# Weighting an expert's output before it is scattered instead of after it is gathered

## The chip, the cores and the metric

The kernel runs on one core of one Trainium2 chip. The metric is the device time of one launch in microseconds. The engines are TensorE (PE, its weight loads PEld), VectorE (DVE), ScalarE (ACT), GpSimd (POOL) and SyncE (SP), which only issues DMAs here. Each engine works through its own list of instructions in order; between engines there are semaphores alone. POOL and SP both issue DMAs, POOL those that scatter rows by an index.

## The reference, cut to what matters

Input x is 4 x 1024 tokens of 256 features in fp32. The kernel computes x + attention(xn) * silu(moe(xn)), with xn the layer norm of x. The mixture of experts is what the change touches:

```python
probs = softmax(x @ gate_w)                      # 8 experts
gate_score, gate_idx = top_k(probs, 2)
gate_score = gate_score / sum(gate_score)
combine = einsum('tk,tke->te', gate_score, onehot) * alpha
h = gelu(einsum('th,ehi->eti', x, fc1_w) + fc1_b)
y = einsum('eti,eih->eth', h, fc2_w) + fc2_b
out = einsum('eth,te->th', y, combine)
```

So each token has two experts, and its output is the sum of their two outputs, each with one weight (score times the expert's alpha). The weight can be multiplied in anywhere after the second bias and before the sum.

## The kernel before, in words

Everything is written out by hand for each engine; no scheduler or planner changes the order. A tile is 128 tokens (rows on the partitions) of 256 features; there are 32 tiles of tokens.

**Attention**, up to about 521 us of the profiled execution, is a sequence of windows (one for four heads of one batch element), in which PE, ACT and DVE share the work. Beside it POOL routes the tokens: it puts the two weights of each token in `weight` (L830) and the two slots in `slot` (L839), and scatters each normalised token twice into `xs_dram`, grouped by expert (`scatter`, L867 to L879). A row of `xs_dram` is 257 words: word 0 is the row of `y_dram` to which the expert's output goes back, copied ahead of the features by L871, and 256 words are the features. Rows that pad an expert's last tile lead to spare rows of `y_dram`.

**The expert loop** runs over 71 tiles of 128 grouped rows (`SLOTS`). SP loads a tile (`load_tile`, L663, four buffers `x_move`). For a tile n, PE transposes it (L1672), ACT takes it to SBUF (L1000), PE makes the hidden layer (L1689), DVE adds the first bias (`h_evacuate`, L1365), ACT does the gelu (L1004), PE makes the output (L1711), DVE adds the second bias (`y_evacuate`, L1405), and POOL scatters the 128 rows into `y_dram` by their row numbers (L903). DVE copies the row numbers out of a tile's buffer (`take_row`, L1359), and only then may SP load the tile four further into that buffer (L662). The loop is skewed: in one round DVE does `take_row(n+3)`, `h_evacuate(n+2)`, `y_evacuate(n)`, and PE transposes n+3, makes the hidden layer of n+2 and the output of n. `ysb` holds eight output tiles; a ninth waits until the first is stored. POOL also multiplies the attention output by inverse sums in 24 of the 71 rounds (`normalise`, L859).

**The last stage** works on 16 pairs of token tiles. `y_dram` has a token's two expert rows side by side. When all scatters have landed, SP loads eight pairs of `ya` (L703) and issues each further load in turn with the stores of the result (L717), behind the waits for `gsum_done` and `fin_done`. For a pair m, ACT multiplies the first expert's rows by their weight into `gsum` (`scale_first`, L1031, two instructions, two pairs ahead of the silu); DVE multiplies the second by its weight and adds (`add_second`, L1420, two instructions); ACT does the silu (L1037); PE has meanwhile made the output projection of attention in one of four banks (L1732, L1737); DVE multiplies the two (`product`, L1430) and adds x (`add_input`, L1435); SP stores. DVE's order in a round is `product(m)`, `add_second(m+2)`, `add_input(m)`. PE may begin pair m once `product(m-4)` has freed its bank.

Of the kernel before, what the change touches and what calls it, by code (L numbers as in the profile page):

```python
# [11 lines left out]

P = 128
B, T, D = 4, 1024, 256
W = D + 1
H, HD = 16, 16
E = 8
KT = D // P
# [129 lines left out]
CH = 4  # L148
# [75 lines left out]
    return isinstance(q, int) and q == NQ - 1  # L224


def in_turn(ahead, what):

    for m in range(AHEAD_OF_PRODUCT):
        ahead(m)  # L230
    for m in range(NT // 2):
        what(m)
        if m + AHEAD_OF_PRODUCT < NT // 2:
            ahead(m + AHEAD_OF_PRODUCT)


def attention_moe_kernel(nc, x, wqT, wkT, wvT, woT, qb, kb, vb, ob, gate, w1, b1, w2, b2, alpha,
                         ident_f, ident_b, mask_neg, mask_negT, before, k_rows, q_rows, numbers, empty_rows, out):
    x_t = x.rearrange("b (t p) d -> p (b t) d", p=P)
# [3 lines left out]
    with ctx:  # L243
# [48 lines left out]
        weight = sb("weight", [P, NT, 2])  # L292
        slot = sb("slot", [P, NT, 2], i32)
        tile_expert = sb("tile_expert", [P, SLOTS], i32)
        y_row_of = sb("y_row_of", [P, SLOTS], i32)
        y_row = sb("y_row", [P, NT, 2], i32)
        blank = sb("blank", [P, W])
        zeros = blank[:, 1:W]
        pad_slot = sb("pad_slot", [P, E], i32)
        spare_f = sb("spare_f", [P, E, 2])  # L300
        spare = sb("spare", [P, E, 2], i32)
        ARENA = 16 * 1024 + CH
        arena = sb("arena", [P, ARENA])
        at = [0]

# [50 lines left out]
        b1_sb = cut(E * D).rearrange("p (e n) -> p e n", e=E)  # L356
        b2_sb = cut(E * D).rearrange("p (e n) -> p e n", e=E)
        at[0] = 0
        xg = [x_move[:, j, 1:W] for j in range(CH)]
        at[0] = 0  # L360
        xgT = [cut(D) for _ in range(CH)]
        w1_now = [cut(KT * D).rearrange("p (k n) -> p k n", k=KT) for _ in range(2)]
# [91 lines left out]
        xg_in = [sem(f"xg_in{n}") for n in range(CH)]  # L454
        t1_done = sem("t1_done"); xgT_out = sem("xgT_out"); l1_done = sem("l1_done"); h_out = sem("h_out")
        g_done = sem("g_done"); w1_ready = sem("w1_ready"); l2_done = sem("l2_done")
        y_out = sem("y_out"); y_stored = [sem(f"y_stored{n}") for n in range(STEP)]
        x_all_in = sem("x_all_in"); a_in = [sem(f"a_in{b}") for b in range(B)]
        ya_in = [sem(f"ya_in{n}") for n in range(DEEP_Y)]
        vb_turned = sem("vb_turned"); vb_out = sem("vb_out"); vb_done = sem("vb_done"); ob_step = sem("ob_step"); ob_split = sem("ob_split"); s_proj = sem("s_proj"); y_scaled = sem("y_scaled")  # L460
        gsum_done = sem("gsum_done"); silu_done = sem("silu_done"); sg_done = sem("sg_done")
        fin_done = sem("fin_done"); stored = sem("stored")

# [19 lines left out]
            return bass.AP(ap.tensor, ap.offset, [list(ap.ap[0]), [0, n]] + [list(x) for x in ap.ap[1:]])  # L483

        def many_zeros(n):
            return bass.AP(zeros.tensor, zeros.offset, [list(zeros.ap[0]), [0, n], [1, D]])

        best, first, second, gap, gexp, where, norm, low = col

# [230 lines left out]

        @block.gpsimd
        def _(pool):
            nc.gpsimd.memset(zeros, 0.0).then_inc(zeros_set, 1)
            for rows in (key_rows, query_rows):
                nc.gpsimd.memset(rows[:, :], 0.0).then_inc(masks_clear, 1)
            pool.wait_ge(masks_clear, 2)
# [140 lines left out]
            def scatter(q, k):  # L867
                r = q - MOVE_FROM
                first_tile, count = MOVES[r], MOVES[r + 1] - MOVES[r]
                pool.wait_ge(scattered, 16 * (2 * first_tile + k * count))  # L870
                nc.gpsimd.tensor_copy(x_move[:, 0:count, 0:1].bitcast(i32),  # L871
                                      y_row[:, first_tile:first_tile + count, k:k + 1]).then_inc(rows_ready, 1)
                pool.wait_ge(rows_ready, 2 * r + k + 2)
                for s in range(count):
                    pool.wait_ge(exp_done, NU * q + BETWEEN_BATCHES[k][s] + SCORE_BANKS + 1)
                    nc.gpsimd.indirect_dma_start(  # L876
                        out=xs_dram, in_=x_move[:, s, :], in_offset=None,
                        out_offset=bass.IndirectOffsetOnAxis(ap=slot[:, first_tile + s, k:k + 1], axis=0)
                        ).then_inc(scattered, 16)  # L879

            for q in range(MOVE_FROM, NQ - 1):
                r = q - MOVE_FROM
                if q > MOVE_FROM and q <= FIRST_TAIL:
                    scatter(q - 1, 1)
                    pool.wait_ge(scattered, 16 * 2 * MOVES[r])
                if q < FIRST_TAIL:
                    first_tile, count = MOVES[r], MOVES[r + 1] - MOVES[r]
                    pool.dma_start(x_move[:, 0:count, 1:W], xn_t[:, first_tile:first_tile + count, :]).then_inc(x_moved, 16)
                next_v(q, q % AUG)
                if PADS_FROM <= q < PADS_FROM + E:  # L890
                    clear_pads(q - PADS_FROM, q)
                if q < FIRST_TAIL:
                    pool.wait_ge(x_moved, 16 * r + 16)
                    scatter(q, 0)
# [3 lines left out]
            for n in range(SLOTS):  # L898
                if n in NORMALISE_BESIDE:
                    normalise(*NORMALISE_BESIDE[n])  # L900
                pool.wait_ge(row_taken, n + 1)
                pool.wait_ge(y_out, n + 3)
                nc.gpsimd.indirect_dma_start(  # L903
                    out=y_dram, in_=ysb[n % STEP], in_offset=None,
                    out_offset=bass.IndirectOffsetOnAxis(ap=y_row_of[:, n:n + 1], axis=0)).then_inc(y_stored[n % STEP], 16)


        @block.scalar
        def _(act):
# [112 lines left out]

            nc.scalar.activation(std[:, :], veps[:, :], ACT.Silu)

            def scale_first(m):
                j = m % DEEP
                act.wait_ge(ya_in[m % DEEP_Y], 16 * (m // DEEP_Y) + 16)
                if m >= DEEP:
                    act.wait_ge(sg_done, m - DEEP + 1)
                for i in range(2):  # L1030
                    ins = nc.scalar.activation(gsum[j][:, i * D:(i + 1) * D], ya[m % DEEP_Y][:, i, 0, :], ACT.Identity,  # L1031
                                               scale=weight[:, 2 * m + i, 0:1])
                ins.then_inc(y_scaled, 1)

            def silu(m):
                act.wait_ge(gsum_done, m + 1)
                nc.scalar.activation(gsum[m % DEEP], gsum[m % DEEP], ACT.Silu).then_inc(silu_done, 1)  # L1037

            in_turn(scale_first, silu)


        @block.vector
        def _(dve):
            dve.sem_inc(piece_used, PIECE_BANKS)
            dve.sem_inc(h_out, 2)
            dve.sem_inc(y_out, 2)

            def statistics(i, b, c):
                if i == 1:
# [306 lines left out]

            def take_row(n, j):
                dve.wait_ge(xg_in[j % CH], 16 * (n // CH) + 16)
                nc.vector.tensor_copy(y_row_of[:, bass.ds(n, 1)], x_move[:, j % CH, 0:1].bitcast(i32)).then_inc(row_taken, 1)  # L1359


            def h_evacuate(n, j):
# [31 lines left out]
            def y_evacuate(n, j):  # L1394
                if n == INVERT_BESIDE:
                    dve.wait_ge(sums_in, 32)
                    invert_sums(B - 1)
                if n == TURN_BIAS + 2:
                    dve.wait_ge(vb_turned, 1)
                    nc.vector.tensor_copy(vb_wide, bank(4)[:, 0:D]).then_inc(vb_out, 1)  # L1400
                e = dve.value_load(tile_expert[0:1, bass.ds(n, 1)], min_val=0, max_val=E - 1)
                dve.wait_ge(l2_done, n + 1)
                if n >= STEP:
                    dve.wait_ge(y_stored[j % STEP], 16 * (n // STEP))
                nc.vector.tensor_tensor(ysb[j % STEP], bank(6 + j % 2)[:, 0:D], b2_sb[:, e, :], ALU.add).then_inc(y_out, 1)  # L1405
                if n >= SPLIT_BESIDE:
                    next(splitting, None)

# [5 lines left out]

            def add_second(m):
                j = m % DEEP
                dve.wait_ge(y_scaled, m + 1)
                for i in range(2):
                    part = gsum[j][:, i * D:(i + 1) * D]
                    ins = nc.vector.scalar_tensor_tensor(part, ya[m % DEEP_Y][:, i, 1, :], weight[:, 2 * m + i, 1:2],  # L1420
                                                         part, ALU.mult, ALU.add)
                ins.then_inc(gsum_done, 1)

            def product(m):
                j = m % DEEP
# [23 lines left out]
        def _(pe):  # L1449
# [244 lines left out]
            def expert_out(n, j):  # L1694
                e = chosen[2]
                if n == 0:
                    pe.wait_ge(o_out, 2 * NQ)
                if n == TURN_BIAS:
                    for k in range(KT):
                        ins = nc.tensor.transpose(bank(4)[:, k * P:(k + 1) * P], vb_sb[:, k * P:(k + 1) * P], idf[:, :])  # L1700
                    ins.then_inc(vb_turned, 1)
                if n == TURN_BIAS + 4:
                    pe.wait_ge(vb_out, 1)
                    for k in range(KT):
                        ins = nc.tensor.matmul(bank(5)[:, 0:D], vb_wide[:, k * P:(k + 1) * P], wo_sb[:, k, :],
                                               start=(k == 0), stop=(k == KT - 1))
                    ins.then_inc(vb_done, 1)
                pe.wait_ge(g_done, n + 1)
                pe.wait_ge(y_out, n + 1)
# [15 lines left out]
            pe.wait_ge(y_out, SLOTS + 2)  # L1725
# [80 lines left out]
```

## Time and profile before

| what | us |
|---|---|
| three runs | 709.43, 714.72, 719.42 |
| median of the runs | 714.72 |
| the profiled execution | 710.94 |
| its span, first to last instruction | 709.1 |
| expert loop in it, from about | 521 |
| last expert tile's bias add on DVE | 664.1 |
| first pair of the last stage reaches ACT | 672.7 |

The profiled execution's own time is 1.84 us longer than its span. Times in the views are microseconds from the start of the span. An engine's "idle before" is how long it stood still ahead of an instruction, with what ended the wait. Durations of successive DVE instructions overlap a little, since one starts while the other drains; so the cost of one in a full queue is the distance from its start to the next start.

### The profile page before, as it was taken

Reading aid. Unit: us, or ns where it says so; the run is one execution under the profiler, and the core shown is the slowest. Engines: PE = TensorE matmul, PEld = TensorE weight load, DVE = VectorE, ACT = ScalarE, POOL = GpSimd, SP = SyncE. Lnnn points to the kernel's source line nnn. Section 1 sums busy time; section 2 is a strip of 40 time slices with the busy share of each in tenths; the row PEclk is TensorE's granted clock in tenths of the full one; section 3 lists DMA queues with packets and bytes.
Section 4 is the critical chain, followed back from the end, with each engine's and each line's share of the span. In section 5 each row is a group of like instructions: output and inputs, shape, how many; then the busy total and the mean of one; then the engine's idle time right before and its main releaser. Section 6 shows DMA issues by size and latency. Waiting matters only on the chain.

```text
span 709.1 us, 17536 instructions
## 1 busy us (share of the span) xinstructions
PE 681.8 (96%) x6039; PEld 461.3 (65%) x6042; DVE 536.7 (76%) x1146; ACT 484.6 (68%) x994; POOL 236.1 (33%) x336
## 2 busy tenths in 40 slices
PE   6998999999999999999999999999999999999885
PEld 3885676455555556555555655554479899999764
DVE  6566988899989988898998998997234654444298
ACT  4552345577877777778787777778876666666374
POOL 5331211242023424333342332200035847575300
PEclk9999999999999999999999999999999999999998
DMA  6999895063485576477568558710279686955396
GB/s 210 313 246 372 294 286 183 9 103 83 78 167 136 139 172 156 132 142 171 130 137 173 135 140 149 158 55 19 62 185 295 215 218 206 238 179 173 117 400 247
DMA packets 74903, 124.46 MB, mean 176 GB/s; under 512 B 14184, under 2 KB 44392, under 8 KB 74696
## 3 DMA queue, kind: packets, MB, share of 16 engines
q1 hardware_dynamic: 65200, 95.17, 52.9%
q0 software_dynamic: 9616, 28.17, 12.7%
q8 instruction: 49, 0.80, 0.5%
q14 instruction: 38, 0.31, 0.2%
HBM read 72.56 MB, written 49.72 MB: 172 GB/s over the span
## 4 chain that ended last, share of the span: by engine, by line
PE 76%; DVE 11%; DMA 7%; ACT 3%; issue 2%; SPq 1%; POOL 0%; DVEq 0%; POOLq 0%; ACTq 0%
PE ps L1600 18%; PE ps L1531 13%; PE ps L1584 12%; PE ps L1689 8%; PE ps L1711 8%; PE ps L1520 6%; PE ps L1480 4%; DVE mxa L1122 4%; DMA q_parts<-arena 2%; PE ps L1490 2%; PE ps L1672 2%; ACT arena L983 2%; DVE x_room L1435 1%; DVE arena L1430 1%; DVE arena L1420 1%
## 5 line engine op out<-in xcount | busy, mean ns | idle before, releaser
L1122 DVE TENSOR_REDUCE mxa<-ps 128x1 f32<-128x512 f32 (+3 forms) x608 | 358.5, 656 | 35.0 <-PE ps L1520 18.9
L983 ACT ACTIVATE arena<-ps 128x512 f32<-128x512 f32 x576 | 303.4, 605 | 80.5 <-PE ps L1584 41.2
L1531 PE MATMUL ps<-aug 57*128 57x512 f32 (+3 forms) x768 | 219.4, 401 | 3.2 <-DVE mxa L1122 1.1
L1584 PE MATMUL ps<-aug 59*128 59x512 f32 (+3 forms) x768 | 216.3, 398 | 0.9 <-ACT arena L983 0.5
L1584 PEld LDWEIGHTS ps<-aug 59*128 59x128 f32 x768 | 110.4, 185 | 77.1 <-ACT arena L983 69.6
L1600 PE MATMUL ps<-arena,v_q 128*32 128x512 f32 (+3 forms) x1536 | 154.5, 497 | 0.9 <-ACT arena L983 0.9
L1531 PEld LDWEIGHTS ps<-aug 57*128 57x128 f32 x768 | 109.9, 185 | 39.8 <-DVE mxa L1122 25.1
L876 POOL DMA_INDIRECT xs_dram<-arena,slot x64 | 62.6, 978 | 76.3 <-ACT arena L983 72.5
L903 POOL DMA_INDIRECT y_dram<-arena,y_row_of x71 | 69.4, 978 | 47.9 <-DVE y_row_of L1359 39.5
L1520 PE MATMUL ps<-key_mask,key_rows 64*128 64x64 bf16 (+2 forms) x704 | 79.1, 208 | 0.0
L1520 PE MATMUL ps<-query_mask,query_rows 64*128 64x128 bf16 (+1 forms) x640 | 75.4, 211 | 0.0
L1689 PE MATMUL ps<-arena 128*128 128x128 f32 x568 | 75.2, 275 | 0.0
L1711 PE MATMUL ps<-w_sb,arena 128*128 x284 | 73.1, 380 | 0.0
L1689 PEld LDWEIGHTS ps<-arena 128*128 128x128 f32 x568 | 69.1, 192 | 0.5 <-issue 0.4
L1365 DVE TENSOR_TENSOR arena<-ps,arena 128x256 f32<-128x256 f32 x71 | 30.1, 424 | 39.5 <-PE ps L1689 39.3
L1011 ACT ACTIVATE arena<-w_sb 128x512 f32 x69 | 43.5, 630 | 20.9 <-issue 19.6
L1405 DVE TENSOR_TENSOR arena<-ps,arena 128x256 f32<-128x256 f32 x71 | 30.1, 424 | 33.0 <-PE ps L1711 32.9
L1600 PEld LDWEIGHTS ps<-arena,v_q 128*32 128x32 f32 x1536 | 34.5, 108 | 31.3 <-issue 18.1
L1480 PE MATMUL ps<-split_room 128*128 128x512 f32 x192 | 52.7, 409 | 1.1 <-DVE split_room L1181 1.1
L1711 PEld LDWEIGHTS ps<-w_sb,arena 128*128 128x128 f32 x284 | 48.7, 191 | 4.2 <-issue 0.4
L1004 ACT ACTIVATE arena<-arena 128x256 f32<-128x256 f32 x71 | 29.6, 417 | 27.5 <-DVE arena L1365 27.5
L1520 PEld LDWEIGHTS ps<-key_mask,key_rows 64*128 64x128 bf16 x704 | 36.5, 96 | 18.2 <-issue 8.9
(149 smaller groups left out, 641.3 us busy)
## 6 DMA issues: line engine op xcount, KB each, us to landing
aug<-k_parts SPq DMA_DIRECT2D x96, 128.0 KB
aug<-q_parts SPq DMA_DIRECT2D x96, 128.0 KB
arena<-xs_dram SPq DMA_DIRECT2D x71, 128.5 KB, 2.6
k_parts<-arena SPq DMA_DIRECT2D x16, 512.0 KB, 6.2
q_parts<-arena SPq DMA_DIRECT2D x16, 512.0 KB, 5.9
arena<-y_dram SPq DMA_DIRECT2D x16, 512.0 KB, 6.8
xn_dram<-arena SPq DMA_DIRECT2D x8, 512.0 KB, 7.3
a_dram<-arena SPq DMA_DIRECT2D x128, 32.0 KB
```

Of the source, the lines that this page charges most:

```text
L876: nc.gpsimd.indirect_dma_start(out=xs_dram, in_=x_move[:, s, :], in_offset=None, out_offset=bass.IndirectOffsetOnAxis(ap=slot[:, first_til ...
L903: nc.gpsimd.indirect_dma_start(out=y_dram, in_=ysb[n % STEP], in_offset=None, out_offset=bass.IndirectOffsetOnAxis(ap=y_row_of[:, n:n + 1] ...
L983: nc.scalar.activation(prob_slot(q, i), score_bank(q, i), ACT.Exp).then_inc(exp_done, 1)
L1011: nc.scalar.activation(w1_now[j % 2], w1_sb[:, bass.ds(e * KT, KT), :], ACT.Copy).then_inc(w1_ready, 1)
L1122: nc.vector.tensor_reduce(dst, src, AX.X, ALU.max).then_inc(piece_used, 1)
L1480: ins = nc.tensor.matmul(bank(4 + n % 2), w[:, k, m * P:(m + 1) * P], xT[:, k, :], start=(s == 0 and k == 0), stop=(s == 2 and k == KT - 1))
L1520: ins = nc.tensor.matmul(dst, stationary[rows, :], over(mask[rows, :], count), start=False, stop=(half == 1))
L1531: ins = nc.tensor.matmul(banks[:, at_ * width:(at_ + 1) * width], k_aug[n][rows, hp, ib * P:(ib + 1) * P], q_aug[n][rows, hp, lo:lo + widt ...
L1584: ins = nc.tensor.matmul(out_[:, col0:col0 + hi - lo], q_aug[n][rows, h // SIDES_OF_ARRAY, jb * P:(jb + 1) * P], k_aug[n][rows, h // SIDES ...
L1600: ins = nc.tensor.matmul(bank(OUT_BANK)[2 * HD * h:2 * HD * (h + 1), lo - c * BANK:BANK], v_q[n][:, jb, h, :], prob_slot(q, i)[:, col0:col ...
L1689: ins = nc.tensor.matmul(bank(2 + j % 2)[:, m * P:(m + 1) * P], w1_now[j % 2][:, k, m * P:(m + 1) * P], xgT[j % CH][:, k * P:(k + 1) * P], ...
L1711: ins = nc.tensor.matmul(bank(6 + j % 2)[:, 0:D], hid[j % CH][:, k * P:(k + 1) * P], w2_sb[:, e * KT + k, :], start=(k == 0), stop=(k == K ...
```

## The change

The row that travels through `xs_dram` has two leading words instead of one (`LEAD = 2`, a row of 258 words): the row number, and the weight of this token for this expert. POOL writes the second with one more small copy for each scatter group. `take_row` copies both words out, into `row_and_weight`, which lies in the room of `logits`. `y_evacuate` adds the bias as before (its semaphore is now `y_biased`, for which PE and the DVE itself wait), and then multiplies the tile in place by the row's weight; only then POOL may scatter it (`y_out`). In the last stage ACT's two scalings of a pair are gone, and DVE adds the pair's two gathered rows with one instruction of 512 columns.

```diff
-W = D + 1
+LEAD = 2
+W = D + LEAD
...
+                nc.gpsimd.tensor_copy(x_move[:, 0:count, 1:2], weight[:, first_tile:first_tile + count, k:k + 1]
+                                      ).then_inc(rows_ready, 1)
+                pool.wait_ge(rows_ready, 2 * (2 * r + k) + 3)
...
-                pool.wait_ge(y_out, n + 3)
+                pool.wait_ge(y_out, n + 1)
...
-            def scale_first(m):
-                j = m % DEEP
-                act.wait_ge(ya_in[m % DEEP_Y], 16 * (m // DEEP_Y) + 16)
-                if m >= DEEP:
-                    act.wait_ge(sg_done, m - DEEP + 1)
-                for i in range(2):
-                    ins = nc.scalar.activation(gsum[j][:, i * D:(i + 1) * D], ya[m % DEEP_Y][:, i, 0, :], ACT.Identity,
-                                               scale=weight[:, 2 * m + i, 0:1])
-                ins.then_inc(y_scaled, 1)
...
-                nc.vector.tensor_copy(y_row_of[:, bass.ds(n, 1)], x_move[:, j % CH, 0:1].bitcast(i32)).then_inc(row_taken, 1)
+                nc.vector.tensor_copy(row_and_weight[:, n, :], x_move[:, j % CH, 0:LEAD].bitcast(i32)).then_inc(row_taken, 1)
...
-                nc.vector.tensor_tensor(ysb[j % STEP], bank(6 + j % 2)[:, 0:D], b2_sb[:, e, :], ALU.add).then_inc(y_out, 1)
+                nc.vector.tensor_tensor(ysb[j % STEP], bank(6 + j % 2)[:, 0:D], b2_sb[:, e, :], ALU.add).then_inc(y_biased, 1)
+                dve.wait_ge(y_biased, n + 3)
+                nc.vector.tensor_scalar(ysb[j % STEP], ysb[j % STEP], row_and_weight[:, n, 1:2].bitcast(fp32), None,
+                                        ALU.mult).then_inc(y_out, 1)
...
             def add_second(m):
                 j = m % DEEP
-                dve.wait_ge(y_scaled, m + 1)
-                for i in range(2):
-                    part = gsum[j][:, i * D:(i + 1) * D]
-                    ins = nc.vector.scalar_tensor_tensor(part, ya[m % DEEP_Y][:, i, 1, :], weight[:, 2 * m + i, 1:2],
-                                                         part, ALU.mult, ALU.add)
-                ins.then_inc(gsum_done, 1)
+                dve.wait_ge(ya_in[m % DEEP_Y], 16 * (m // DEEP_Y) + 16)
+                if m >= DEEP:
+                    dve.wait_ge(sg_done, m - DEEP + 1)
+                nc.vector.tensor_tensor(gsum[j].rearrange("p (t d) -> p t d", d=D), ya[m % DEEP_Y][:, :, 0, :],
+                                        ya[m % DEEP_Y][:, :, 1, :], ALU.add).then_inc(gsum_done, 1)
```

One round of the expert loop on DVE, before: `ISA` and `TENSOR_LOAD` rows read the tile's expert into a register.

```order
L1401 TENSOR_LOAD tile_expert
L1401 ISA x2
L1405 ISA
L1405 TENSOR_TENSOR arena<-ps,arena 128x256
L1359 COPY y_row_of<-arena 128x1
L1363 TENSOR_LOAD tile_expert
L1363 ISA x2
L1365 ISA
L1365 TENSOR_TENSOR arena<-ps,arena 128x256
```

The same round now (`logits` is the room of the rows and weights; L1390 is the bias add, L1350 the hidden layer's):

```order
L1386 TENSOR_LOAD tile_expert
L1386 ISA x2
L1390 ISA
L1390 TENSOR_TENSOR arena<-ps,arena 128x256
L1392 TENSOR_SCALAR arena<-arena,logits 128x256
L1344 COPY logits<-arena 128x2
L1348 TENSOR_LOAD tile_expert
L1348 ISA x2
L1350 ISA
L1350 TENSOR_TENSOR arena<-ps,arena 128x256
```

The weighting stands between the bias add and the copy of the next tile's leading words, 71 times.

The end of the loop and the start of the last stage on DVE, before:

```order
L1405 TENSOR_TENSOR arena<-ps,arena 128x256
L1420 SCALAR_TENSOR_TENSOR arena<-arena,weight 128x256 x4
L1430 TENSOR_TENSOR arena<-ps,arena 128x512
L1420 SCALAR_TENSOR_TENSOR arena<-arena,weight 128x256 x2
L1435 TENSOR_TENSOR x_room<-x_room,arena 128x512
```

and now:

```order
L1390 TENSOR_TENSOR arena<-ps,arena 128x256
L1392 TENSOR_SCALAR arena<-arena,logits 128x256
L1408 TENSOR_TENSOR arena<-arena 128x512 x2
L1417 TENSOR_TENSOR arena<-ps,arena 128x512
L1408 TENSOR_TENSOR arena<-arena 128x512
L1422 TENSOR_TENSOR x_room<-x_room,arena 128x512
```

Four instructions ahead of the first product have become two, and two in each round have become one. PE's list is unchanged.

## Rows read from the trace of the kernel before

**Rows 1.** Page, chain that ended last, by engine

```profile
PE 76%; DVE 11%; DMA 7%; ACT 3%; issue 2%; SPq 1%; POOL 0%; DVEq 0%; POOLq 0%; ACTq 0%
```

**Rows 2.** Timeline, expert loop: start us, us, engine, line; in brackets idle before

```profile
541.19 0.42 DVE L1405 TENSOR_TENSOR arena<-ps,arena 128x256 f32<-128x256 f32 x1 [0.44 <-PE ps L1711]
...
541.53 0.14 DVE L1359 COPY y_row_of<-arena 128x1 int32<-128x1 int32 x1
...
542.30 0.42 DVE L1365 TENSOR_TENSOR arena<-ps,arena 128x256 f32<-128x256 f32 x1 [0.62 <-PE ps L1689]
542.37 0.97 POOL L903 DMA_INDIRECT y_dram<-arena,y_row_of  x1 [1.01 <-DVE y_row_of L1359]
```

**Rows 3.** Chain of waits and timeline where PE waits for a tile

```profile
549.98 7.12 DMA arena<-xs_dram
...
557.15 0.44 PE L1672 MATMUL ps<-idf,arena 128*128 128x128 f32 x2 [0.30 <-DMA arena<-xs_dram]
```

**Rows 4.** Single lines: duration ns min/median/max, first and last start us, shapes

```profile
L1171 DVE TENSOR_SCALAR arena<-arena,rstd,shift x2: 408/411/414, 6.6 to 6.9; 128x256 f32<-128x256 f32 x2
L1342 DVE COPY arena<-w_sb x2: 427/428/428, 517.7 to 518.5; 128x512 f32 x2
L871 POOL COPY arena<-y_row x22: 187/188/214, 177.4 to 452.8; 128x3 int32<-128x3 int32 x20, 128x2 int32<-128x2 int32 x2
```

**Rows 5.** Timeline, DVE and POOL in a round with a normalise

```profile
561.73 0.74 POOL L859 TENSOR_TENSOR v_all<-v_all,arena 128x256 f32<-128x256 f32 x1
561.83 0.80 DVE L1377 CAST arena<-ob_sb 128x256 bf16<-128x256 f32 x1
```

**Rows 6.** Timeline, end of the expert loop: DVE and POOL

```profile
662.12 0.42 DVE L1405 TENSOR_TENSOR arena<-ps,arena 128x256 f32<-128x256 f32 x1 [0.44 <-PE ps L1711]
...
663.30 0.96 POOL L903 DMA_INDIRECT y_dram<-arena,y_row_of  x1 [0.80 <-DVE arena L1405]
...
665.83 0.96 POOL L903 DMA_INDIRECT y_dram<-arena,y_row_of  x1 [0.30 <-issue]
```

**Rows 7.** Timeline of DVE in the last stage

```profile
675.73 0.69 DVE L1430 TENSOR_TENSOR arena<-ps,arena 128x512 f32<-128x512 f32 x1
...
681.92 0.68 DVE L1430 TENSOR_TENSOR arena<-ps,arena 128x512 f32<-128x512 f32 x1
682.52 0.87 DVE L1420 SCALAR_TENSOR_TENSOR arena<-arena,weight 128x256 f32<-128x256 f32 x2
683.30 0.69 DVE L1435 TENSOR_TENSOR x_room<-x_room,arena 128x512 f32<-128x512 f32 x1
683.91 0.69 DVE L1430 TENSOR_TENSOR arena<-ps,arena 128x512 f32<-128x512 f32 x1
...
703.81 0.70 DVE L1430 TENSOR_TENSOR arena<-ps,arena 128x512 f32<-128x512 f32 x1
704.54 0.69 DVE L1435 TENSOR_TENSOR x_room<-x_room,arena 128x512 f32<-128x512 f32 x1
```

**Rows 8.** Timeline of ACT in the last stage

```profile
672.70 0.91 ACT L1031 ACTIVATE arena<-arena,weight 128x256 f32<-128x256 f32 x2 [9.05 <-DMA arena<-y_dram]
674.00 0.91 ACT L1031 ACTIVATE arena<-arena,weight 128x256 f32<-128x256 f32 x2 [0.38 <-DMA arena<-y_dram]
674.81 0.61 ACT L1037 ACTIVATE arena<-arena 128x512 f32<-128x512 f32 x1
675.60 0.91 ACT L1031 ACTIVATE arena<-arena,weight 128x256 f32<-128x256 f32 x2 [0.17 <-DMA arena<-y_dram]
```

**Rows 9.** Timeline of PE in the last stage

```profile
676.56 0.55 PE L1732 MATMUL ps<-arena,before_sb 128*128 128x512 bf16 x1 [4.05 <-DVE arena L1430]
...
699.83 1.89 PE L1737 MATMUL ps<-wo_sb,v_all 128*128 128x256 f32 x8
```

**Rows 10.** DMA issues: size and median us to landing, whole span

```profile
arena<-y_dram SPq DMA_DIRECT2D x16, 512.0 KB, 6.8
```

**Rows 11.** Table by stretch: busy us (count) by engine, PEclk, DMA share, GB/s

```profile
690.00:695.00 5.00, 4.95 (x24) 4.22 (x24) 5.00 (x11) 3.69 (x9) 0.00 (x0) 1.00 1.07 398
```

More of the change, by code:

```diff
@@ L224, in is_last @@
     return isinstance(q, int) and q == NQ - 1
[L227 to L234, printed above, removed]
 def attention_moe_kernel(nc, x, wqT, wkT, wvT, woT, qb, kb, vb, ob, gate, w1, b1, w2, b2, alpha,
@@ L294, in attention_moe_kernel @@
         tile_expert = sb("tile_expert", [P, SLOTS], i32)
-        y_row_of = sb("y_row_of", [P, SLOTS], i32)
+        row_and_weight = logits[:, :, :].rearrange("p t e -> p (t e)")[:, 0:LEAD * SLOTS].bitcast(i32).rearrange("p (n r) -> p n r", r=LEAD)
         y_row = sb("y_row", [P, NT, 2], i32)
         blank = sb("blank", [P, W])
-        zeros = blank[:, 1:W]
+        zeros = blank[:, LEAD:W]
         pad_slot = sb("pad_slot", [P, E], i32)
@@ L301, in attention_moe_kernel @@
         spare = sb("spare", [P, E, 2], i32)
-        ARENA = 16 * 1024 + CH
+        ARENA = 16 * 1024 + LEAD * CH
         arena = sb("arena", [P, ARENA])
@@ L358, in attention_moe_kernel @@
         at[0] = 0
-        xg = [x_move[:, j, 1:W] for j in range(CH)]
+        xg = [x_move[:, j, LEAD:W] for j in range(CH)]
         at[0] = 0
@@ L456, in attention_moe_kernel @@
         g_done = sem("g_done"); w1_ready = sem("w1_ready"); l2_done = sem("l2_done")
-        y_out = sem("y_out"); y_stored = [sem(f"y_stored{n}") for n in range(STEP)]
+        y_biased = sem("y_biased"); y_out = sem("y_out"); y_stored = [sem(f"y_stored{n}") for n in range(STEP)]
         x_all_in = sem("x_all_in"); a_in = [sem(f"a_in{b}") for b in range(B)]
         ya_in = [sem(f"ya_in{n}") for n in range(DEEP_Y)]
-        vb_turned = sem("vb_turned"); vb_out = sem("vb_out"); vb_done = sem("vb_done"); ob_step = sem("ob_step"); ob_split = sem("ob_split"); s_proj = sem("s_proj"); y_scaled = sem("y_scaled")
+        vb_turned = sem("vb_turned"); vb_out = sem("vb_out"); vb_done = sem("vb_done"); ob_step = sem("ob_step"); ob_split = sem("ob_split"); s_proj = sem("s_proj");
         gsum_done = sem("gsum_done"); silu_done = sem("silu_done"); sg_done = sem("sg_done")
@@ L485, in many_zeros @@
         def many_zeros(n):
-            return bass.AP(zeros.tensor, zeros.offset, [list(zeros.ap[0]), [0, n], [1, D]])
+            first = blank[:, 1:W]
+            return bass.AP(first.tensor, first.offset, [list(first.ap[0]), [0, n], [1, W - 1]])
         best, first, second, gap, gexp, where, norm, low = col
@@ L722, in _ @@
         def _(pool):
-            nc.gpsimd.memset(zeros, 0.0).then_inc(zeros_set, 1)
+            nc.gpsimd.memset(blank[:, 1:W], 0.0).then_inc(zeros_set, 1)
             for rows in (key_rows, query_rows):
@@ L872, in scatter @@
                                       y_row[:, first_tile:first_tile + count, k:k + 1]).then_inc(rows_ready, 1)
-                pool.wait_ge(rows_ready, 2 * r + k + 2)
+                nc.gpsimd.tensor_copy(x_move[:, 0:count, 1:2], weight[:, first_tile:first_tile + count, k:k + 1]
+                                      ).then_inc(rows_ready, 1)
+                pool.wait_ge(rows_ready, 2 * (2 * r + k) + 3)
                 for s in range(count):
@@ L887, in _ @@
                     first_tile, count = MOVES[r], MOVES[r + 1] - MOVES[r]
-                    pool.dma_start(x_move[:, 0:count, 1:W], xn_t[:, first_tile:first_tile + count, :]).then_inc(x_moved, 16)
+                    pool.dma_start(x_move[:, 0:count, LEAD:W], xn_t[:, first_tile:first_tile + count, :]).then_inc(x_moved, 16)
                 next_v(q, q % AUG)
@@ L901, in _ @@
                 pool.wait_ge(row_taken, n + 1)
-                pool.wait_ge(y_out, n + 3)
+                pool.wait_ge(y_out, n + 1)
                 nc.gpsimd.indirect_dma_start(
                     out=y_dram, in_=ysb[n % STEP], in_offset=None,
-                    out_offset=bass.IndirectOffsetOnAxis(ap=y_row_of[:, n:n + 1], axis=0)).then_inc(y_stored[n % STEP], 16)
+                    out_offset=bass.IndirectOffsetOnAxis(ap=row_and_weight[:, n, 0:1], axis=0)).then_inc(y_stored[n % STEP], 16)
         @block.scalar
@@ L1037, in silu @@
                 nc.scalar.activation(gsum[m % DEEP], gsum[m % DEEP], ACT.Silu).then_inc(silu_done, 1)
-            in_turn(scale_first, silu)
+            for m in range(NT // 2):
+                silu(m)
         @block.vector
@@ L1045, in _ @@
             dve.sem_inc(h_out, 2)
-            dve.sem_inc(y_out, 2)
+            dve.sem_inc(y_biased, 2)
             def statistics(i, b, c):
@@ L1708, in expert_out @@
                 pe.wait_ge(g_done, n + 1)
-                pe.wait_ge(y_out, n + 1)
+                pe.wait_ge(y_biased, n + 1)
                 for k in range(KT):
@@ L1723, in _ @@
             skewed(((x_transpose, 3), (hidden, 2), (second_expert, 0), (expert_out, 0)), 0)
-            pe.wait_ge(y_out, SLOTS + 2)
+            pe.wait_ge(y_biased, SLOTS + 2)
             pe.wait_ge(ob_split, NBIAS)
```

## Prediction, made blind

> **What bounds the kernel now.** I read the chain of waits first. It is three quarters PE [rows 1]: attention and the expert loop run at PE's pace, and DVE's share lies in the last stage. So I asked, stage by stage, which engine has no idle time.
>
> In the expert loop PE has none; a round takes 1.98 us, and DVE stands still twice in it, 0.44 us before the output's bias add and 0.62 us before the hidden layer's [rows 2], together 1.06 us. Work added on DVE there is hidden as long as it stays under that. PE's one wait in the middle of the loop is 0.30 us for a tile load that took 7.12 us [rows 3]; by SP's list it waits for a `take_row` on DVE, so what delays `take_row` can delay it.
>
> In the last stage DVE has no idle time. A round is product, two halves of `add_second`, `add_input`, with starts 0.60, 0.78 and 0.61 us apart, 1.99 us in all [rows 7]. Two others are nearly as full: PE does its twelve late pairs from 676.56 to 701.72 [rows 9], 1.9 us each after a first of 3.8 at the lower clock, and the DMA moves 398 GB/s [rows 11].
>
> **The last stage, which gains.** The one new instruction of 512 columns has two fp32 operands in SBUF, as `add_input` has, whose start-to-start cost is 0.61 us; I take 0.60. It replaces 0.78. A round becomes 1.80 us. The start moves too. Today load 0 lands and ACT begins at 672.70, load 1 at 674.00 and load 2 at 675.60 [rows 8], and DVE's first product comes at 675.73 because it sits behind ACT's scaling and the adds of both pairs. With ACT out: add 0 at 672.7, add 1 at 674.0, silu 0 (0.61 us [rows 8]) done by 674.2, product 0 at 674.6; add 2 when its load lands, 675.65; `add_input` 0 at 676.25; product 1 at 676.85. Then 1.80 us a round: product 14 at 676.85 + 13 x 1.80 = 700.25, against 703.81 [rows 7]. What follows product 14 is the same list in both. Gain 3.56 us.
>
> Three covers have to hold for that.
> - PE: pair 4 starts after product 0, so 1.13 us earlier, and the last pair is done at 700.6 instead of 701.72. Product 15 comes 1.33 us after product 14 (0.73 us between an instruction and one that waits for it, as from 703.81 to 704.54 [rows 7], and 0.60), at 701.58. Slack 1.0 us.
> - Loads: 512 KB each [rows 10], stores half that. After load 0, which lands at 672.70 [rows 8], 15 more loads and 7 stores have to move until load 15 is in, 9.7 MB; at 398 GB/s [rows 11] that is 24.4 us, 697.1. It is needed at 699.05. A load is issued some 10.9 us before its use at the new pace, and the median landing takes 6.8 [rows 10].
> - ACT has a single silu of 0.61 us in 1.80.
>
> **The expert loop, which pays.** The weighting is a 128x256 fp32 tensor_scalar in SBUF with a scalar from SBUF; the nearest row is L1171, the same form, 0.41 us [rows 4]. With 0.03 us for DVE's wait on its own bias add (704.54 less the end of 703.81's 0.70 [rows 7]) it adds 0.44 us between a tile's bias add and both its scatter and `take_row`. The lower bound is half of L1171, if both halves of a row go at once, as the 128x512 copy in 0.43 us suggests [rows 4]: 0.24 us. The upper bound is the cast of 128x256 that took 0.80 us beside POOL's normalise [rows 5]: 0.83 us. I take 0.44, since L1171 is the same operation.
>
> The trace shows the copy L1342 twice as fast per column as L1171. The Trainium skill, "VectorE: DVE Perf Modes", section "The perf-mode tier table", puts `tensor_scalar` on fp32 in SBUF in the same double-speed class as `tensor_copy`. By it the weighting would be near the lower bound and the sum 0.4 us better; this case's L1171 speaks against it, though it has two operations and not one.
>
> - DVE's load: 0.44 us out of 1.06 idle. It goes into the 0.62 us before L1365, so neither evacuation starts later. PE now waits for `y_biased`, which is as early as `y_out` was. Cost 0. Were the 0.62 exceeded, L1365 would be late, and the gelu behind it, but PE needs it two rounds later.
> - POOL's scatters: each can start 0.44 us later, POOL idles 1.01 before each [rows 2]; `ysb` has eight buffers. Cost 0 in the loop. At the end it is on the path: the last four scatters are queued on POOL 1.27 us apart from the one at 663.30, which waited for the bias add at 662.12 [rows 6]; its wait grows by 0.44, the last one (665.83) goes with it, and the loads of the last stage wait for all of them. Cost +0.44 us (0.24 to 0.83).
> - `take_row` and with it the load of the tile four further: 0.44 us later. Covered except in the stretch where landing takes 7 us; there PE's wait of 0.30 [rows 3] becomes 0.74. Cost +0.44 us. Bounds: 0 if the DMA queue, not the issue, sets that landing; +1.3 if three such loads in a row are late.
>
> **Edits that cost nothing.** 22 more copies on POOL of 0.19 us [rows 4], between waits for attention's ACT and for scatters to land, tens of us in all; without that cover they would be 4 us of POOL time, which no engine waits for. A row of 258 words instead of 257: 0.4% more on tile loads. ACT loses 32 scalings, which were not the bound once the first had been done. The leading words are copied two at a time instead of one, in the same 0.14 us [rows 2].
>
> **Sum.** -3.56 + 0.44 + 0.44 = -2.7 us: the profiled execution's 710.94 us becomes 708.2. Bounds: -3.56 + 0.24 + 0 = -3.3; with only the earlier start gained (-1.1) and both costs high, +1.0.
>
> **Rivals.**
> 1. *The last stage keeps its pace.* Loads or PE step in where DVE gets faster: three resources within 3% of each other. For it: PE's slack of 1.0 us and 398 GB/s already moved, where 1.80 us a round would ask for 437. Against it: the head start of eight loads and the 2 us by which load 15 is early. Only the start's 1.1 us is gained, net -0.2: 710.7 on the profiled scale. Chance 0.22.
> 2. *The weighting waits for POOL.* Rows 5 show a DVE cast that began 0.10 us after a POOL tensor_tensor and finished 0.16 us after it, 0.80 us for what alone would take at most 0.43. If the weighting is of that kind, it takes up to 0.80 us in the 24 rounds with a normalise, still under 1.06. After the last normalise it runs beside nothing but the tail of a scatter. Net -2.7 to -1.9. Chance 0.13. The Trainium skill, "SBUF — State Buffer", section "Who interferes with whom", says that a `tensor_scalar` in a two-port mode and a GpSimd instruction exclude each other for the whole instruction, whichever came first. Rows 5 agree with that for a cast.
> 3. *Slower.* The same exclusion, but each weighting waits out a whole scatter issue on POOL (0.97 us) and then runs: 0.03 + 0.97 + 0.41 = 1.41 us a round, against 1.06 of idle. It decides from 1.06 us on: 0.35 x 71 = 25 us slower, 733 on the profiled scale. Against it: the scatter of a tile starts only 0.76 us after the bias add (541.61 to 542.37 [rows 2]), and would start later still, so that by the next weighting (543.6) no more than 0.2 us of it is left. Chance 0.04.
> 4. *Late tiles.* The loop in which a slow load, `take_row` and the issue follow one another grows by 0.44 us every four tiles in the dozen rounds around this wait: up to 1.3 us instead of 0.44. Net -1.8. Chance 0.08.
>
> The forecast itself has 0.53.
>
> **The numbers.** 2% is 14 us, which is also about what a measurement of this kernel tells from no change; nothing but rival 3 reaches it. The four executions shown (709.43, 710.94, 714.72, 719.42) spread wider than the effect: their middle is 712.8, the profiled one lies below it and 3.8 below the median. Taking 2.7 from 712.8 I forecast 710 us. The range: lowest run less 3.3 is 706, highest plus 1.0 is 720, and a median seldom sits at either end; I take 705 to 718. Chances: faster 0.02, within 2% 0.94, slower 0.04.
>
> **What would show it.** In the profile after: starts of successive products 1.80 us apart and DVE without idle time (right), or with waits on `arena<-y_dram` or PE (rival 1); the first product about 1.9 us after the first load has landed, now 3.0; the weighting at 0.41 us everywhere (right), at 0.2 to 0.3 alone and 0.8 beside L859's successor (rival 2), over 1 us (rival 3); no idle time of PE before L1711's successor; the wait in the middle of the loop up from 0.30 to about 0.7. I am wrong if the last stage, from the first load's landing to the end, is not 3 to 4 us shorter than its 36.4.

## The result: 1.56% slower, and why a full engine looked half idle

Over four runs the changed kernel took a median of 724.34 us (719.77 to 726.95), the kernel before 714.31 us (709.43 to 719.42): a ratio of 1.0156, 95% interval 1.0111 to 1.0201. That is outside the forecast range. The ratio lies within the 2% to which the prediction gave 0.94, but on the other side of 1 than the forecast gain. The last stage gained nearly what was forecast; the expert loop lost five times as much. Milestones of the two profiled executions, us:

| stretch | before | changed | difference |
|---|---|---|---|
| start to the loop's first output bias add | 526.35 | 527.56 | +1.2 |
| loop, first to last output bias add | 137.74 | 154.46 | +16.7 |
| to the first landed load of the last stage | 8.61 | 8.26 | -0.35 |
| last stage, from there to the end | 36.40 | 33.22 | -3.2 |
| span | 709.1 | 723.5 | +14.4 |

The changed kernel's chain of waits, by engine, against [rows 1]:

```profile
PE 58%; DVE 20%; DMA 8%; issue 6%; DVEq 5%; ACT 2%; SPq 1%; POOL 0%; POOLq 0%; ACTq 0%
```

PE has lost 18 points. DVE has gained 9, and "issue" and DVEq, the instructions that DVE's sequencer runs without its datapath, have gained 9 together.

The last stage in the changed kernel, timeline of DVE (start us, us, engine, line; L1408 is the sum of two rows, L1417 the product, L1422 the addition of x), answering [rows 7]:

```profile
690.28 0.69 DVE L1408 TENSOR_TENSOR arena<-arena 128x512 f32<-128x512 f32 x1 [7.45 <-DMA arena<-y_dram]
691.57 0.69 DVE L1408 TENSOR_TENSOR arena<-arena 128x512 f32<-128x512 f32 x1 [0.59 <-DMA arena<-y_dram]
692.17 0.68 DVE L1417 TENSOR_TENSOR arena<-ps,arena 128x512 f32<-128x512 f32 x1
693.58 0.69 DVE L1408 TENSOR_TENSOR arena<-arena 128x512 f32<-128x512 f32 x1 [0.72 <-DMA arena<-y_dram]
...
698.39 0.68 DVE L1417 TENSOR_TENSOR arena<-ps,arena 128x512 f32<-128x512 f32 x1
698.99 0.68 DVE L1408 TENSOR_TENSOR arena<-arena 128x512 f32<-128x512 f32 x1
699.59 0.68 DVE L1422 TENSOR_TENSOR x_room<-x_room,arena 128x512 f32<-128x512 f32 x1
700.20 0.68 DVE L1417 TENSOR_TENSOR arena<-ps,arena 128x512 f32<-128x512 f32 x1
```

The first product comes 1.89 us after the first landed load, and a round takes 1.81 us: both as forecast (1.9 and 1.80), with no wait on PE or DMA behind the third load's.

One round of the expert loop in the changed kernel, timeline of DVE (L1390 output bias, L1392 weighting, L1344 copy of the two words, L1350 hidden bias), answering [rows 2]:

```profile
587.09 0.42 DVE L1350 TENSOR_TENSOR arena<-ps,arena 128x256 f32<-128x256 f32 x1 [0.34 <-issue]
...
587.95 0.42 DVE L1390 TENSOR_TENSOR arena<-ps,arena 128x256 f32<-128x256 f32 x1 [0.43 <-issue]
...
588.41 0.35 DVE L1392 TENSOR_SCALAR arena<-arena,logits 128x256 f32<-128x256 f32 x1
588.68 0.16 DVE L1344 COPY logits<-arena 128x2 int32<-128x2 int32 x1
...
589.17 0.42 DVE L1350 TENSOR_TENSOR arena<-ps,arena 128x256 f32<-128x256 f32 x1 [0.34 <-issue]
```

A round is 2.08 us from 587.09 to 589.17, and DVE still shows 0.77 us of idle time in it. But the releaser is no longer PE: it is "issue", time in which nothing in the profile is waited for. The chain of waits of the same round (start us, us, what) shows what fills it:

```profile
587.09 0.34 DVE arena L1350
587.43 0.04 issue
587.47 0.19 DVEq L1386
587.66 0.03 issue
587.69 0.02 DVEq L1386
587.72 0.05 issue
587.76 0.02 DVEq L1389
587.79 0.05 issue
587.83 0.07 DVEq L1390
587.90 0.05 issue
587.95 0.44 DVE arena L1390
```

L1386 is the load of the tile's expert number into a register: TENSOR_LOAD, 0.30 us, which starts right behind the start of the hidden layer's bias add and runs beneath it, then 0.19 us of register operations and a check of 0.02. Only when the address is formed (L1390, 0.07) is the next add issued. The chain's first row, 0.34 us, is the time until the load is done. So it is steps of the sequencer, one after another, that set the distance between the two adds.

The kernel before had it too, hidden behind waits that name PE. The rows that tell it are those of a round in which DVE came late and caught up, timeline of DVE in the kernel before:

```profile
611.26 0.43 DVE L1405 TENSOR_TENSOR arena<-ps,arena 128x256 f32<-128x256 f32 x1 [0.78 <-PE ps L1711]
611.61 0.14 DVE L1359 COPY y_row_of<-arena 128x1 int32<-128x1 int32 x1
612.07 0.42 DVE L1365 TENSOR_TENSOR arena<-ps,arena 128x256 f32<-128x256 f32 x1 [0.32 <-PE ps L1689]
612.91 0.42 DVE L1405 TENSOR_TENSOR arena<-ps,arena 128x256 f32<-128x256 f32 x1 [0.42 <-PE ps L1711]
```

Here a round takes 1.65 us, and none was shorter in that trace until PE's last tiles. That is DVE's full round: 0.81 us from the output's bias add to the hidden layer's, and 0.84 back. Its room under PE's 1.98 was 0.33 us and not 1.06.

In the changed kernel's round above the way back is nearly the same, 0.86, and the first part has grown from 0.81 to 1.22 us (587.95 to 589.17). The register load for the hidden layer's bias shows why. This is that load in the round before and in the changed one (ns min/median/max, first and last start us):

```profile
L1363 DVEq TENSOR_LOAD <-tile_expert x1: 298/298/298, 611.3 to 611.3; - x1
```

```profile
L1348 DVEq TENSOR_LOAD <-tile_expert x1: 302/302/302, 588.4 to 588.4; - x1
```

Before, it starts 0.06 us after the output's bias add (611.26). In the changed kernel it stands behind the weighting in DVE's list, and the weighting waits until the bias add is done (587.95 to 588.41), so the load starts 0.48 us after that add; both are also the medians over the rounds. From the load's start to the hidden layer's add it is 0.75 us in both. So a round was 0.06 + 0.75 + 0.84 = 1.65 us and is 0.48 + 0.75 + 0.86 = 2.08 (the terms are rounded). The added 0.42 is the wait for the bias add; the weighting's own 0.35 us runs beneath the load and what follows it.

### The profile page after: what moved, and what is told of

It reads as the page before. It is cut to its first block, busy times and chain, and to the rows that moved or that the text cites. A ratio compares the mean times of both kernels' runs of the same rounds, so it can differ in the third digit from the quotient of the medians.

```text
span 723.5 us, 17581 instructions
## 1 busy us (share of the span) xinstructions
PE 693.0 (96%) x6039; PEld 463.1 (64%) x6042; DVE 572.0 (79%) x1201; ACT 471.5 (65%) x962; POOL 240.5 (33%) x358
## 4 chain that ended last, share of the span: by engine, by line
PE 58%; DVE 20%; DMA 8%; issue 6%; DVEq 5%; ACT 2%; SPq 1%; POOL 0%; POOLq 0%; ACTq 0%
PE ps L1587 18%; PE ps L1518 13%; PE ps L1571 12%; PE ps L1507 6%; DVE mxa L1107 5%; PE ps L1467 4%; DVE arena L1390 4%; DVE arena L1392 3%; DVEq L1386 3%; DMA q_parts<-arena 2%; PE ps L1477 2%; DVE arena L1350 2%; DMA arena<-xs_dram 2%; DVE x_room L1422 1%; DVEq L1348 1%
## 5 line engine op out<-in xcount | busy, mean ns | idle before, releaser
L897 POOL DMA_INDIRECT y_dram<-arena,logits x71 | 69.6, 980 | 63.0 <-DVE logits L1344 58.6
L1676 PE MATMUL ps<-arena 128*128 128x128 f32 x568 | 79.1, 282 | 1.8 <-ACT arena L994 1.4
L1698 PE MATMUL ps<-w_sb,arena 128*128 x284 | 75.0, 387 | 0.6 <-DVE arena L1390 0.5
L1390 DVE TENSOR_TENSOR arena<-ps,arena 128x256 f32<-128x256 f32 x71 | 30.0, 423 | 28.1 <-issue 22.9
L1350 DVE TENSOR_TENSOR arena<-ps,arena 128x256 f32<-128x256 f32 x71 | 29.8, 420 | 19.3 <-issue 12.0
```

Source lines behind the costliest of these rows:

```text
L897: nc.gpsimd.indirect_dma_start(out=y_dram, in_=ysb[n % STEP], in_offset=None, out_offset=bass.IndirectOffsetOnAxis(ap=row_and_weight[:, n, ...
L1676: ins = nc.tensor.matmul(bank(2 + j % 2)[:, m * P:(m + 1) * P], w1_now[j % 2][:, k, m * P:(m + 1) * P], xgT[j % CH][:, k * P:(k + 1) * P], ...
```

## The experiments

Theory 1: DVE's round is full, since register loads run in series with its instructions. (The expectations put the full round before at 1.70 us; its rows say 1.65.) Theory 2: tile loads are issued later, and PE waits for tiles. Theory 3: the weighting is locked out by POOL. Ratios are to the kernel before on the same chip, with 95% intervals. The kernel before took medians of 729.29, 711.92 and 726.95 us beside the three groups of runs, so totals are compared only as ratios. "Rounds" are start-to-start times of the output bias add; the sum over the 54 rounds from tile 12 to tile 66 is 106.96 us before and 117.26 changed.

**tail_only**: the kernel before with `scale_first` removed and the new `add_second`.

```diff
-            in_turn(scale_first, silu)
+            for m in range(NT // 2):
+                silu(m)
```

> Only the last stage is changed: rows of 257 words and the expert loop as before, ACT's scaling gone and DVE adds the two rows unweighted, so the output lacks the weights. All theories: the last stage from the first landed load to the end takes 33.2 us, as in the changed kernel, against 36.4 before; rounds of the expert loop stay at 1.98 us; total 3 to 3.6 us under the kernel before.

Ratio 0.994 (0.9901 to 0.9979). Last stage 33.01 us, 54 rounds in 106.84. The last stage's gain is real and comes alone.

**no_weighting**: the changed kernel without L1392; POOL's scatter waits for `y_biased` instead.

```diff
-                dve.wait_ge(y_biased, n + 3)
-                nc.vector.tensor_scalar(ysb[j % STEP], ysb[j % STEP], row_and_weight[:, n, 1:2].bitcast(fp32), None,
-                                        ALU.mult).then_inc(y_out, 1)
```

> The changed kernel without the weighting on DVE in the expert loop (the output lacks the weights); the two-word rows and the new last stage stay. All theories: expert loop back at 1.98 us a round, total 3 to 3.6 us under the kernel before. If the loss came from the wider rows, from POOL's extra copies or from where buffers lie, the total stays near the changed kernel, 10 us above before.

Ratio 0.996 (0.9927 to 0.9994); 54 rounds in 106.86, last stage 33.96 us. Rows of 258 words, POOL's copies and the moved buffers cost nothing that can be seen; the loss is the weighting's.

**one_load**: the changed kernel, one register load of the expert number a round.

```diff
 def h_evacuate(n, j):
-                e = dve.value_load(tile_expert[0:1, bass.ds(n, 1)], min_val=0, max_val=E - 1)
+                e = experts[n] = dve.value_load(tile_expert[0:1, bass.ds(n, 1)], min_val=0, max_val=E - 1)
...
 def y_evacuate(n, j):
-                e = dve.value_load(tile_expert[0:1, bass.ds(n, 1)], min_val=0, max_val=E - 1)
+                e = experts.pop(n)
```

> The changed kernel, but DVE reads a tile's expert number into a register once, for the hidden layer's bias, and keeps it for the output's bias two rounds later. Theory 1 (DVE's round is full: register loads run one after the other with its instructions, show as no busy time, and the weighting pushed the round from 1.70 to 2.08 us): a DVE round needs about 1.6 to 1.7 us, PE sets 1.98 again, total 0 to 3 us under the kernel before. Theory 2 (tile loads issued later) and theory 3 (weighting locked out by POOL): nothing they rest on has changed, total stays 8 to 11 us above before.

Ratio 1.0006 (0.9978 to 1.0035). DVE's busy time is that of the changed kernel, 572.0 us in both pages, and the loss is gone. Timeline of DVE (L1392 output bias, L1394 weighting, L1352 hidden bias):

```profile
603.12 0.42 DVE L1392 TENSOR_TENSOR arena<-ps,arena 128x256 f32<-128x256 f32 x1 [0.33 <-PE ps L1700]
603.58 0.35 DVE L1394 TENSOR_SCALAR arena<-arena,logits 128x256 f32<-128x256 f32 x1
603.85 0.16 DVE L1344 COPY logits<-arena 128x2 int32<-128x2 int32 x1
604.34 0.42 DVE L1352 TENSOR_TENSOR arena<-ps,arena 128x256 f32<-128x256 f32 x1 [0.34 <-PE ps L1678]
605.10 0.42 DVE L1392 TENSOR_TENSOR arena<-ps,arena 128x256 f32<-128x256 f32 x1 [0.33 <-issue]
```

A round is 1.98 us again with the weighting in it; catching-up rounds take 1.53 and 1.61. Theories 2 and 3 fall as the main cause.

**before_third_load**: the kernel before, one more register load and nothing else.

```diff
                 e = dve.value_load(tile_expert[0:1, bass.ds(n, 1)], min_val=0, max_val=E - 1)
+                dve.value_load(tile_expert[0:1, bass.ds(n, 1)], min_val=0, max_val=E - 1)
                 dve.wait_ge(l2_done, n + 1)
```

> The kernel before with one more register load of the expert number on DVE in each round of the expert loop, ahead of the output's bias add, its value unused. No busy time of DVE's datapath is added. Theory 1: DVE's round goes from 1.70 to about 2.1 us, the loop runs at that, total 7 to 10 us above before. Theory 2: take_row is some 0.4 us later, so a wait or two for tiles grows, 1 to 3 us above before, rounds elsewhere 1.98. Theory 3: no change.

Ratio 1.034 (1.0289 to 1.0392), more than theory 1 had said. Timeline of DVE (L1406 output bias):

```profile
636.47 0.42 DVE L1406 TENSOR_TENSOR arena<-ps,arena 128x256 f32<-128x256 f32 x1 [1.03 <-issue]
636.81 0.14 DVE L1359 COPY y_row_of<-arena 128x1 int32<-128x1 int32 x1
637.28 0.42 DVE L1365 TENSOR_TENSOR arena<-ps,arena 128x256 f32<-128x256 f32 x1 [0.33 <-issue]
638.73 0.42 DVE L1406 TENSOR_TENSOR arena<-ps,arena 128x256 f32<-128x256 f32 x1 [1.02 <-issue]
```

A round is 2.26 us while DVE's datapath is busy for 0.98 of it and "idle" for 1.35. One load costs 0.61 us: 1.65 + 0.61 = 2.26. This is theory 1 without any weighting; it had put the load at 0.4 us.

**loop_only**: the changed kernel with `scale_first` and the old `add_second` put back in the last stage.

```diff
-            for m in range(NT // 2):
-                silu(m)
+            in_turn(scale_first, silu)
```

> The changed kernel's two-word rows and weighting in the expert loop, with the last stage of the kernel before (ACT scales, DVE multiplies and adds, so each row is weighted twice and the output differs). Theory 1 (DVE's round is full): rounds of 2.08 us and more as in the changed kernel, last stage 36.4 us from the first landed load, total about 14 us above before, 3 to 4 more than the changed kernel. If the gain of the last stage and the loss of the loop did not add, the total would lie nearer the changed kernel's.

Ratio 1.018 (1.0146 to 1.0213); rounds of 2.08 us, last stage 37.3 us. That agrees with a loss of the loop and a gain of the last stage that add, though the interval just overlaps that of changed_again below.

**row_first**: the weighting behind `take_row` of the next round.

```diff
-            skewed(((take_row, 3), (h_evacuate, 2), (y_evacuate, 0)), -CH)
+            skewed(((take_row, 3), (weigh, -1), (h_evacuate, 2), (y_evacuate, 0)), -CH)
+            weigh(SLOTS - 1, (SLOTS - 1) % STEP)
```

> The changed kernel, but in DVE's list a tile's weighting stands behind take_row of the next round instead of ahead of it, so tile loads are issued as early as in the kernel before. Theory 1: DVE still does the same work in a round, 2.08 us where nothing else holds it, total 10 to 12 us above before. Theory 2 (late tile loads): the long waits for tiles in the first ten rounds are gone and with them most of the loss, total 0 to 5 us above before. Theory 3 (lock with POOL): no change from the changed kernel.

Ratio 1.0105 (1.0062 to 1.0147), 7.5 us and so less than theory 1 expected; 54 rounds in 116.3 us, median round 2.08. Timeline of DVE (L1395 output bias, L1381 weighting):

```profile
655.00 0.42 DVE L1395 TENSOR_TENSOR arena<-ps,arena 128x256 f32<-128x256 f32 x1 [0.43 <-issue]
655.34 0.16 DVE L1344 COPY logits<-arena 128x2 int32<-128x2 int32 x1
655.46 0.35 DVE L1381 TENSOR_SCALAR arena<-arena,logits 128x256 f32<-128x256 f32 x1
656.22 0.42 DVE L1350 TENSOR_TENSOR arena<-ps,arena 128x256 f32<-128x256 f32 x1 [0.41 <-issue]
657.08 0.42 DVE L1395 TENSOR_TENSOR arena<-ps,arena 128x256 f32<-128x256 f32 x1 [0.43 <-issue]
```

The copy stands 0.34 us behind the bias add again, as before the change, and the round is still 2.08 us: the weighting, with its wait for the bias add, still stands ahead of the register load. The first twelve rounds took 27.5 us against 30.1 in the changed kernel, but kernels with the same loop differ there by as much (28.0 in loop_only). By this stretch theory 2 explains at most 3 us.

**psum_weigh**: the weighting reads PSUM.

```diff
-                nc.vector.tensor_tensor(ysb[j % STEP], bank(6 + j % 2)[:, 0:D], b2_sb[:, e, :], ALU.add).then_inc(y_biased, 1)
+                nc.vector.tensor_tensor(bank(6 + j % 2)[:, 0:D], bank(6 + j % 2)[:, 0:D], b2_sb[:, e, :], ALU.add).then_inc(y_biased, 1)
...
-                nc.vector.tensor_scalar(ysb[j % STEP], ysb[j % STEP], row_and_weight[:, n, 1:2].bitcast(fp32), None,
+                nc.vector.tensor_scalar(ysb[j % STEP], bank(6 + j % 2)[:, 0:D], row_and_weight[:, n, 1:2].bitcast(fp32), None,
```

> The changed kernel, but the bias add writes back into its PSUM bank and the weighting reads PSUM and writes the output tile, so it has no SBUF tensor as a source; PE gets the bank 0.45 us later, which it has time for. Theory 3 (the weighting, 0.35 us alone and up to 0.92 beside POOL's normalise, waits for POOL): the weighting takes 0.42 us in every round, also beside the normalise, and if that lock made the loss, the total falls to 0 to 3 us above before. Theory 1: rounds become 2.15 us instead of 2.08, total 2 to 5 us above the changed kernel, though the lock is gone.

Ratio 1.0131 (1.0099 to 1.0164), no different from the changed kernel's 1.0127 and 1.0156. The weighting's line (ns min/median/max), first in the changed kernel and then here:

```profile
L1392 DVE TENSOR_SCALAR arena<-arena,logits x71: 352/354/924, 528.0 to 682.5; 128x256 f32<-128x256 f32 x71
```

```profile
L1392 DVE TENSOR_SCALAR arena<-ps,logits x71: 482/484/486, 530.4 to 681.9; 128x256 f32<-128x256 f32 x71
```

The lock is there in the first (up to 924 ns) and gone in the second, and the time stays, though the copy now comes 0.87 us behind the bias add: a long weighting overlaps with the register work behind it. Theory 3 falls. Rounds were 2.12 us, not 2.15, and the total was not above the changed kernel's, as theory 1 had it.

**changed_again**: the changed kernel, not edited, beside the last group.

> The changed kernel once more, on the same chip as the other three: 10 to 12 us above before, rounds of 2.08 us.

Ratio 1.0127 (1.0095 to 1.0159); 54 rounds in 117.81 us, last stage 32.55 us. The result repeats.

**before_one_load**: the edit of one_load in the kernel before.

> The kernel before with one register load of the expert number a round on DVE instead of two. Its DVE round of 1.70 us is under PE's 1.98 already, so theory 1 gives no change in most rounds and at most 1 us from the few rounds in which DVE was late: within 1 us of before. If register loads on DVE cost time in themselves wherever they stand, it would be some 15 us faster.

Ratio 0.9996 (0.9974 to 1.0017). Where DVE is not the bound a register load is free.

**one_load_row_first**, **one_load_psum** and **one_load_psum_row_first** combine the edits shown, in search of a version that beats both.

> The changed kernel with both: one register load a round on DVE, and the weighting behind take_row. Theory 1: PE's 1.98 us a round, the last stage's gain kept, total 2 to 4 us under the kernel before, at or a little under the version with one load alone, since tile loads go out 0.4 us earlier. Were theory 2 worth more than a wait or two, it would be 3 us or more under that version.

> The changed kernel with one register load a round on DVE and the weighting read from PSUM. So far: the full round of DVE costs most, and the lock with POOL costs the second tile load in the loop's first rounds. If both hold and add: rounds of 1.98 us, no weighting over 0.5 us, the second round at 2.1 to 2.3 us instead of 3.4 to 3.8, total 2 to 4 us under the kernel before. If the lock costs nothing of its own: as one register load alone, within 1 us of before.

> As the version with one register load and the weighting from PSUM, and the weighting stands behind take_row of the next round. If late tile loads still cost something with the lock gone, it is 1 us or more under that version; if not, the two are alike, 3 to 4 us under the kernel before.

Ratios 1.0014 (0.9982 to 1.0046), 0.9989 (0.9961 to 1.0017) and 1.0007 (0.9982 to 1.0032). All run at PE's 1.98 us in the median, and their last stages take 33.87, 32.89 and 33.39 us. None is shown to be faster than the kernel before; the expectation of 2 to 4 us under it failed in all three. Their 54 rounds take 109.65, 109.05 and 107.97 us, 1 to 3 more than before, and the second round was not cured by the PSUM source (3.90 us in one_load_psum).

## Why the prediction was wrong, step by step

- **The last stage, -3.56 us: right.** It measured -3.2 in the changed kernel, the difference being that the third load landed 3.30 us after the first and not 2.95. The stage took 32.6 to 34.0 us in the nine other runs with the new sum, against 36.3 to 37.3 in those with the old one. Its covers held: the last product ran 0.61 us behind the addition before it, and DMA moved 396 GB/s from 710 to 715 us.
- **"DVE's load: 0.44 us out of 1.06 idle. Cost 0": this is the step that failed.** The 1.06 us were read from two idle times whose last releaser was PE. A releaser only says what came last. Within those times DVE's sequencer had work of its own, and the free room was what a late round can catch up, 1.98 less 1.65, or 0.33 us. The weighting needs 0.43. That this is close to the forecast 0.44 is luck: the forecast was the weighting's work, 0.41, and 0.03 of wait; the rows show the wait of the register load behind the weighting for the bias add, with the work beneath the load. Measured: +10.3 us over 54 rounds, of which 0.10 us a round make 5.4.
- **The rest of it is rounds of 2.2 to 2.5 us.** They have two sources. In both kernels DVE's sequencer pauses once in about ten rounds between two register instructions, as here in the chain of waits of the changed kernel:

```profile
593.74 0.19 DVEq L1386
593.93 0.40 issue
594.33 0.02 DVEq L1386
```

  And some register loads take longer than 0.30 us, before and changed (ns min/median/max):

```profile
L1401 DVEq TENSOR_LOAD <-tile_expert x71: 297/303/525, 525.5 to 663.0; - x71
```

```profile
L1386 DVEq TENSOR_LOAD <-tile_expert x71: 299/304/710, 526.8 to 681.2; - x71
```

  Over the 54 rounds of the changed kernel, 12 of 108 loads took over 0.40 us, together 3.1 us more than the median; before, 3 of 107. Before, a round with a pause took 2.3 us and the next one 1.65 to 1.73; with a full round nothing is caught up. What the pause is, and why some loads are long, was not tried.
- **The weighting's own 0.41 us: nearly right**, 0.35, between the two bounds. It is 0.06 us faster than L1171 [rows 4], and from PSUM it takes 0.48. The table of the Trainium skill's "VectorE: DVE Perf Modes", section "The perf-mode tier table", had it in the double-speed class when both ends are in SBUF; the trace agrees in that the SBUF form is the faster, by 0.13 us.
- **`take_row` and the tile loads, +0.44: too small.** The one wait grew to four, 4.8 us together on PE's weight loads from 527 to 556 us, the longest behind this load of a tile in the chain of waits of the changed kernel, answering [rows 3]:

```profile
541.02 9.41 DMA arena<-xs_dram
```

  The first twelve rounds took 30.1 us against 25.1. How much of that is the later issue is open: loops without the weighting took 26.5 to 27.6 in other runs.
- **The last scatter, +0.44: not there.** The stretch from the last bias add to the first landed load fell by 0.35 instead. Three scatters, not four, had stood in a row from 663.30 on. Now the last tiles came 1.3 to 1.6 us apart, only the last scatter was held up by the one before it, and it started 1.71 us after the last bias add (683.73) against 1.74: the shorter queue made up for the weighting. The other 0.32 lies between that scatter and the first landed load, and its cause is open.
- **Rival 3** had the right place and sign, DVE's round as the bound, with the wrong price and the wrong mechanism: its threshold of 1.06 us was the same misread number, and taking the weighting's lock with POOL away (psum_weigh) changed nothing. It was given 0.04.

Open: no run has the weighting behind the register load in DVE's list, or without its wait, which would tell the price of the wait from that of the work; that it is the wait is read from the rows, and row_first and psum_weigh agree with it. And with one load a round the sum of the parts is 3 us under the kernel before, and the ratio is 1. The profiles show 1 to 3 us of it as scattered longer rounds, with later waits for tiles among them; the rest is within the runs' spread.

## What to carry to other kernels

Before costing work at nothing because an engine is idle, find that engine's own minimum: look for a round in which it was late and caught up, and take the distance of its starts there, not the idle time with another engine's name on it. Register loads, address formation and checks count into that minimum though they show no busy time. When a chain of waits turns from engine names to "issue" and the sequencer's rows, take instructions away from the sequencer first: here one load fewer paid for the weighting. And look at what stands behind an instruction that waits for its forerunner on the same engine: here it was a register load, which had run beneath that forerunner.

## What the runs showed of the hardware that was not expected

- A load of a number from SBUF into a register on DVE, with its check and what follows, takes 0.61 us of a full round (2.26 less 1.65); its parts in the chain of before_third_load are 0.30, 0.18 and 0.02 us with gaps of 0.03 to 0.04. It can start 0.06 us after the start of the add ahead of it, and so run beneath it. In a round with room it costs nothing (0.9996).
- A tensor_scalar of 128x256 fp32 took 0.35 us from SBUF and up to 0.92 beside POOL, and 0.48 us from PSUM beside anything. "SBUF — State Buffer" in the Trainium skill, section "Who interferes with whom", says that such instructions and GpSimd's exclude each other; the trace agrees, and in this kernel the blocked time cost nothing, as the sequencer's work went on beneath it.
